# A first stretch unrolled and re-ordered, low weight halves on GpSimd, nine experts' weights prepared beside the first attention groups

## What is computed

```python
x  = L0_attn_x                         # 4 x 1024 x 256, float32: 4096 tokens
xn = layernorm(x)
# attention: 16 heads of 16, causal, q/k/v/o projections with biases
# experts: for each token the 4 best of 16 experts, and 2 shared ones (sw_*: 352 = 2 x 176 columns)
g = einsum('th,ehi->tei', xn, w_gate)  # 16 x 256 x 176
u = einsum('th,ehi->tei', xn, w_up)
y = einsum('tei,eih->th', silu(g) * u * combine, w_down)    # 16 x 176 x 256
y = y + silu(xn @ sw_gate) * (xn @ sw_up) @ sw_down
return x + attention(xn) + y
```

## Time and profile before

| | |
|---|---|
| median of 3 runs | 1188.08 us |
| the profiled execution, its own time | 1197.33 us |
| its span | 1195.7 us |
| PE busy | 1002.8 us (84%) |
| DVE busy | 867.1 us (73%) |
| ACT busy | 654.7 us (55%) |
| POOL busy | 584.0 us (49%) |
| mean granted TensorE clock | 0.934 of full |

### The profile page before, as it was taken

The page is one execution under the profiler, slowest core; times in us unless marked ns, Lnnn a source line. Parts: engine busy times, 40 slices in busy tenths (PEclk is TensorE's granted clock), DMA queues, the critical chain, the costliest instruction groups (busy, mean ns, idle before and its releaser), DMA issues.

```text
span 1195.7 us, 26395 instructions
## 1 busy us (share of the span) xinstructions
PE 1002.8 (84%) x8634; PEld 523.0 (44%) x8634; DVE 867.1 (73%) x1790; ACT 654.7 (55%) x1219; POOL 584.0 (49%) x529
## 2 busy tenths in 40 slices
PE   2877515998989899999998989898989898999875
PEld 1444302444444444554444445444444454444433
DVE  5988687887887767677868776777777766677433
ACT  4777500544545665557666755566666554666431
POOL 6433217777660555346665643565656534544000
PEclk9998755999999999999999999999999998999888
DMA  5998726223242435354544444544444435344602
GB/s 168 286 302 278 233 78 194 62 69 88 68 120 69 97 67 106 52 111 75 107 85 98 87 87 76 91 89 92 78 95 82 99 52 102 58 100 58 136 1 35
DMA packets 99484, 126.41 MB, mean 106 GB/s; under 512 B 24873, under 2 KB 83514, under 8 KB 98834
## 3 DMA queue, kind: packets, MB, share of 16 engines
q0 software_dynamic: 41632, 60.79, 28.4%
q1 hardware_dynamic: 57730, 63.99, 18.0%
HBM read 71.63 MB, written 57.80 MB: 108 GB/s over the span
## 4 chain that ended last, share of the span: by engine, by line
PE 59%; DVE 12%; issue 7%; ACT 2%; SPq 2%; DMA 2%; POOL 0%; ACTq 0%; DVEq 0%
PE gup L1231 12%; PE pvp L1154 12%; PE outs L1258 10%; DVE part L1324 7%; PE smp L1110 6%; PE turn L1243 5%; PE stp L1135 4%; PE outs L1161 4%; PE turn L1201 3%; PE smp L1093 1%; DVE sg L1376 1%; DVE hf L1381 1%; ACT probs L1494 1%; DMA Qs<-nm 1%; DVE probs L1423 1%
## 5 line engine op out<-in xcount | busy, mean ns | idle before, releaser
L1494 ACT ACTIVATE probs<-stp 128x1024 f32<-128x1024 f32 (+1 forms) x320 | 300.1, 938 | 276.6 <-PE stp L1135 267.9
L1324 DVE TENSOR_REDUCE part<-smp 128x2 f32<-128x256 f32 (+2 forms) x372 | 345.8, 950 | 49.5 <-PE smp L1093 30.6
L1231 PE MATMUL gup<-gu_w,XC 128*128 (+1 forms) x1152 | 213.3, 323 | 13.4 <-DVE hf L1381 13.0
L952 POOL DMA_INDIRECT XG<-xrow_d,slots x144 | 147.1, 1022 | 81.6 <-issue 40.2
L959 POOL DMA_INDIRECT out<-Y,slots x72 | 117.2, 1628 | 137.6 <-ACT Y L1527 112.3
L1258 PE MATMUL outs<-dn_w,h 88*128 (+1 forms) x1248 | 183.0, 280 | 0.1
L959 POOL DMA_INDIRECT acc_d<-Y,slots x72 | 115.1, 1599 | 119.5 <-ACT Y L1527 100.9
L1154 PE MATMUL pvp<-probs,Vs 128*32 128x512 f32 (+3 forms) x1536 | 167.8, 509 | 0.8 <-DVE probs L1423 0.7
L941 POOL DMA_INDIRECT slot_d<-entry,slot_i x128 | 129.2, 1009 | 42.5 <-issue 42.5
L1110 PE MATMUL smp<-Ks,Qs 48*128 48x128 f16 (+2 forms) x744 | 112.3, 340 | 38.7 <-DVE part L1324 21.6
L1386 DVE TENSOR_TENSOR h<-turn,h 88x256 f16<-88x256 f32 x208 | 86.6, 417 | 78.3 <-ACT h L1506 77.0
(11 more groups left out here) (174 smaller groups left out, 1138.2 us busy)
## 6 DMA issues: line engine op xcount, KB each, us to landing
rb<-rsum_d SPq DMA_DIRECT2D x60, 128.0 KB
Ks<-k_d SPq DMA_DIRECT2D x96, 64.0 KB
Qs<-q_d SPq DMA_DIRECT2D x96, 64.0 KB
v_d<-V SPq DMA_DIRECT2D x8, 544.0 KB, 5.1
Vs<-v_d SPq DMA_DIRECT2D x16, 272.0 KB, 3.3
acc_d<-YA SPq DMA_DIRECT2D x1, 4224.0 KB
X<-L_attn_x POOLq DMA_DIRECT2D x8, 512.0 KB, 4.8
xrow_d<-XR SPq DMA_DIRECT2D x8, 512.0 KB, 5.0
```

The costliest lines, as they stand in the source:

```text
L952: pool.indirect_dma_start(XG[:, q].rearrange("p a c t -> p (a c t)"), None, s.xrow_d, bass.IndirectOffsetOnAxis(ap=slots[:, r, 0:1], axis= ...
L1231: last = pe.matmul(gup[:, 0:2 * I], columns[:, a, h], weights_of(s.gu_w, e, b, h, slice(0, 2 * I)), start=n == 0, stop=n == 5)
L1324: last = dve.tensor_reduce(part[:, g % 2, k0 // CH, :, j, t], banks[:, :, col:col + w], AX.X, ALU.max)
L1494: act.activation(to, of, ACT.Exp, scale=float(DK) ** -0.5 / QS ** 2).then_inc(exp_done, 1)
```

## The change

- **Order in `prepare`.** All eight chunks are written out; there is no loop. Rows are normalised two chunks ahead and variances taken three ahead: `normalise(c+2)` and `rows_low(c+2)`, and at the end of step `c` `variances(c+3)` on DVE and `root(c+3)` on ACT. Rows 0 and 1 and the variances of 2 stand ahead of the first step. ACT's first work is now the scaling of Wq and Wk; `root(0)` comes behind it.
- **Weights in `prepare`.** Only `s.EARLY` = 7 experts and the 2 shared ones, one expert a step (`c - 1` in step `c`), at the end of ACT's step. The low halves are made by POOL with four instructions in place of DVE's two.
- **The other nine** (`LATER`) are prepared in the third stage, one every five slots, from slot 2 on: SP loads each into the space of `XG` or `YA`, ACT makes the high halves and DVE the low halves. `XG` and `YA`, and the first routed unit on PE, wait for the last of them (`wlo_done`).
- The clearing of `Ks` (one memset of 128x6144 on POOL before) is cut into six of 1024 elements, three in steps 0 and 1 and three in steps 6 and 7.

```diff
@@ prepare, gpsimd @@
+            def weights_low(e, n, k):
+                (gh, gl), (dh, dl) = expert_parts(e)
+                pool.wait_ge(hi_made, 2 * k + 1)
+                pool.tensor_scalar(gu[:, n], gu[:, n], WS, None, ALU.mult).then_inc(scaled, 1)
+                pool.wait_ge(hi_made, 2 * k + 2)
+                pool.tensor_scalar(dn[:, n], dn[:, n], WS, None, ALU.mult).then_inc(scaled, 1)
+                pool.wait_ge(scaled, 2 * k + 1)
+                pool.tensor_tensor(gl, gu[:, n], gh, ALU.subtract).then_inc(lo_made, 1)
+                pool.wait_ge(scaled, 2 * k + 2)
+                pool.tensor_tensor(dl, dn[:, n], dh, ALU.subtract).then_inc(lo_made, 1)
...
-            pool.memset(s.Ks[:, :, :, :], ONES).then_inc(k_ones, 1)
+            def step(c):
+                if c + 4 < NCH:
+                    load_x(c + 4)
+                if c < 2 or c >= NCH - 2:
+                    for b in range(c % 2, NB, 2):
+                        pool.memset(s.Ks[:, b, 0 if c < 2 else 1], ONES).then_inc(k_ones, 1)
+                if c == 0:
+                    for n in range(SH):
+                        weights_low(E + n, n, n)
+                else:
+                    weights_low(c - 1, (c - 1) % 2, c + 1)
+                for e in (range(2) if c == 0 else (c + 1,) if c + 1 < s.EARLY else ()):
+                    pool.wait_ge(lo_made, 2 * (e + 1))
+                    load_expert(e % 2, s.w_gate[e], s.w_up[e], s.w_down[e])
@@ prepare, scalar @@
-            def step(c, p, first, last):
-                product(c, 0)
-                product(c, 1)
-                if more(p, last):
-                    root(c + 1)
-                    rows_high(c + 1, 1 - p)
-                weights_high(c, 0)
-                product(c, 2)
-                product(c, 3)
-                if more(p, last):
-                    columns(c + 1, 1 - p)
+            def step(c):
+                for i in range(4):
+                    product(c, i)
+                if later(c, 2) is not None:
+                    rows_high(c + 2)
                 act.wait_ge(lg_done, c + 1)
...
+                if later(c, 1) is not None:
+                    columns(c + 1)
+                if c == 0:
+                    for n in range(SH):
+                        weights_high(E + n, n, 1)
+                else:
+                    weights_high(c - 1, (c - 1) % 2, (c - 1) // 2 + 2)
+                if later(c, 3) is not None:
+                    root(c + 3)
...
-            root(0)
             act.wait_ge(w_in, 48)
...
             act.activation(w16[:, 2, 0], w32[:, 2], ACT.Copy, scale=WS).then_inc(w_hi, 1)
+            root(0)
+            rows_high(0)
+            columns(0)
+            root(1)
+            rows_high(1)
             act.wait_ge(gt_out, 1)
             act.activation(g16[:, 0], gT32[:, :, :], ACT.Copy, scale=WS).then_inc(w_hi, 1)
+            root(2)
@@ prepare, vector @@
+            def step(c):
+                ahead = later(c, 2) is not None
                 low_half(c, 0)
+                if ahead:
+                    normalise(c + 2)
+                for i in range(1, 4):
+                    low_half(c, i)
+                if ahead:
+                    rows_low(c + 2)
                 values(c, 0)
                 values(c, 1)
+                if later(c, 3) is not None:
+                    variances(c + 3)
@@ attention_and_experts @@
+        WEIGHTS_FROM, WEIGHTS_STEP = 2, 5
+        LATER = E - s.EARLY
+        def weights_at(g, n, half):
+            k = g * SLOTS + n - WEIGHTS_FROM - 2 * half
+            return k // WEIGHTS_STEP if k >= 0 and k % WEIGHTS_STEP == 0 and k // WEIGHTS_STEP < LATER else None
@@ gpsimd, ahead of the first gather @@
+            pool.wait_ge(wlo_done, 2 * LATER)
@@ sync: load_weights(0) ahead of send_max(0), then at the end of a slot @@
+                    e = weights_at(g, n, 0)
+                    if e is not None and e + 1 < LATER:
+                        load_weights(e + 1)
@@ vector, in a slot behind the unit's work (scalar: the same with n, and weights_high) @@
+                    for half in range(2):
+                        if weights_at(g, n - 1, half) is not None:
+                            weights_low(weights_at(g, n - 1, half), half)
```

More of the change, by code:

```diff
@@ L206, in flat, with one, expert_parts, later @@
             return w.rearrange("p c n -> p (c n)")
[L208 to L221, removed]
+        def one(t):
+            return t.rearrange("p o c n -> p (o c) n")
+        def expert_parts(e):
+            e = slice(e, e + 1) if isinstance(e, int) else bass.ds(e, 1)
+            return ([one(s.gu_w[:, e, a]).rearrange("p c (a i) -> p c a i", a=2) for a in range(2)],
+                    [one(s.dn_w[:, e, a]) for a in range(2)])
+        def later(c, ahead):
+            return c + ahead if c + ahead < NCH else None
         @block.sync
@@ L266, in _ @@
-            over_steps(sp, step)
+            for c in range(2):
+                store_rows(c)
+            for c in range(NCH):
+                step(c)
             sp.wait_ge(wo_in, 16 * (4 * HG + 1))
-            sp.wait_ge(xr_st, 16 * NCH)
-            sp.wait_ge(xt_st, 16 * NCH)
+            for p in range(2):
+                sp.wait_ge(xr_st[p], 8 * NCH)
+                sp.wait_ge(xt_st[p], 8 * NCH)
             for i in range(4):
@@ L522, in _, with turn @@
             dve.tensor_scalar(bqk[:, :, :], bqk[:, :, :], QS, None, ALU.mult).then_inc(b_scaled, 1)
+            variances(2)
             dve.wait_ge(v_ones, 1)
-            rows_low(0, 0)
-            for n in range(SH):
-                weights_low(None, n)
-            over_steps(dve, step)
+            for c in range(NCH):
+                step(c)
         @block.tensor
         def _(pe):
-            def turn(c, p):
+            def turn(c):
                 for j in range(TPC):
                     pe.wait_ge(xlo, TPC * c + j + 1)
-                    if j == 0 and not (isinstance(c, int) and c == 0):
+                    if j == 0 and c:
                         pe.wait_ge(xt_done, TPC * c)
@@ L540, in turn, with step @@
                             last = pe.transpose(tp[j // 2][:, j % 2, o:o + P],
-                                                XR[:, p, j, a, h * P:(h + 1) * P], s.ident16[:, :])
+                                                XR[:, c % 2, j, a, h * P:(h + 1) * P], s.ident16[:, :])
                     last.then_inc(turned, 1)
-            def step(c, p, first, last):
-                began = not (isinstance(c, int) and c == 0)
+            def step(c):
+                p = c % 2
                 pe.wait_ge(xt_done, TPC * (c + 1))
@@ L557, in step @@
                     x.then_inc(qk_done, 1)
-                if more(p, last):
-                    turn(c + 1, 1 - p)
-                if began:
+                if later(c, 1) is not None:
+                    turn(c + 1)
+                if c:
                     pe.wait_ge(lg_out, c)
@@ L584, in _ @@
             last.then_inc(gt_done, 1)
-            turn(0, 0)
             pe.wait_ge(w_lo, 4)
-            over_steps(pe, step)
+            for c in range(NCH):
+                step(c)
 def route(nc, s):
@@ L1540, in _ @@
                         second_half(z)
+                    for half in range(2):
+                        if weights_at(g, n, half) is not None:
+                            weights_high(weights_at(g, n, half), half)
 _INS = ["L0_attn_x", "L0_attn_Wq", "L0_attn_bq", "L0_attn_Wk", "L0_attn_bk", "L0_attn_Wv", "L0_attn_bv",
```

210 lines of the change are left out of this document (103 added, 107 removed).

## The result

| | before | after |
|---|---|---|
| median | 1187.76 us (6 runs, 1181.78 to 1190.33) | 1203.76 us (6 runs, 1198.43 to 1209.56) |
| the profiled execution | 1197.33 us | 1202.95 us |
| its span | 1195.7 us | 1201.0 us |

The ratio is 1.0134, 95% interval 1.0104 to 1.0165: the changed kernel is 16 us slower. The forecast was 1189, no change. All ratios in this document are of fast executions; one execution of experiment 3, of 2291 us, is left out of its ratio.

A forecast was written before the change was run, and what follows sets the result against it. DVE was taken to bound the first stage, PE the third with DVE close behind. -6 and +7 gave +1 on the profiled 1197.33 us, in proportion to the median 1189 us, no change; range 1178 to 1200.

The forecast's parts named there:

- -6 for the first stage: First stage: 4.3 us gained in steps 1 to 5, 4.3 in step 6, 0.3 lost in step 7, 2.5 at the start.
- 0.7 on average: Steps 1 to 5: `re_` on DVE waits 0.7 us a step for POOL's arithmetic, upper case 2.
- rival C: First stage: POOL's lock holds `re_` and DVE's subtractions, steps 14.5 to 15 us, nothing gained there; 1195 us, chance 0.12.
- The end stays: End of the first stage: the store of v and the barrier take as long as before.
- Steps 1 to 5: First stage: 13.4 us for each of these steps, 67.0 against 71.3, so 4.3 us gained.
- The root chain: Steps 1 to 5: statistics, then ACT's root, delay the first q/k product; PE waits 1.85 us for a bank.
- Steps 6 and 7: First stage: step 6 takes 11.0 us against 15.3, having neither root nor rows; step 7 PE's 9.0 plus 0.3.
- The start: Start of the first stage: root's end near 16.1 us, first q/k product at 28.1 against 25.58, 2.5 lost.
- The third stage: Nine late experts cost 7 us: 5 on DVE, 1 on ACT, 1 for SP's issues; bounds 1 and 14.
- the first 45 slots take the same time as before: Third stage: a sign that the forecast is wrong; it expected PE idle about 17 us and groups of 65 us.
- 40% of DVE's: Third stage: the share of DVE's added 12.6 us for nine late experts taken as cost, 5 us.
- D: First stage: the root chain doesn't bind, a step is PE's 11.2 to 12 us, 12 to 15 gained; 1182, chance 0.15.

The follow-up runs named there:

- experiment 3: The kernel before, with the nine late experts prepared a second time in the third stage, same values: 1192.24 us, ratio 1.004.
- experiment 1: The changed kernel with the early experts' low halves back on DVE and no arithmetic on POOL: 1177.48 us, ratio to before 0.9916.
- experiment 4: Low halves on DVE as in experiment 1, with ACT's root behind the second q/k product and DVE's normalising behind the second subtraction: 1170.74 us, ratio 0.9863.
- Experiments 5 and 6: Experiment 5 has its own line; 6 is experiment 4 plus four POOL memsets of an unused tile where the changed kernel has its arithmetic: 1188.07 us, ratio 1.0009.
- Experiment 5: The changed kernel, low halves still on POOL, with experiment 4's order of root and normalising: 1197.42 us, ratio 1.0078.

## Why the prediction was wrong, by its own steps

The forecast was -6 for the first stage and +7 for the third. The profiles show +7.9 for the first; the third's share was measured at +5 (1 to 9). Together 13 of the 16 us; the rest is inside the interval of the ratio (12 to 20 us). The two profiled executions alone are 5 us apart: from the first maxima to the end the one before took 998.3 us, the changed one 995.7. Single executions of one kernel differ by some 10 us, so these two don't measure the third stage.

**The step that failed: "since one of 704 elements is nearer to DVE's 0.8 for that shape I take 0.7 on average".** That is the term for POOL's arithmetic, 3.5 us in all, put on one instruction, `re_`. The runs put POOL's arithmetic at 25.2 us (experiment 1 against the changed kernel). Three things in that step were wrong.

- The size. POOL does not take DVE's time for the shape. An expert is 6.6 us on POOL, against 1.4 on DVE. The estimate that I had from the Trainium skill's page GPSIMD Engine Reference, section 3.1, 1.5 us for the subtraction of 704, was right (1.51 measured), and I left it out of the sum. The scaling, which no row priced, took more, 1.97.
- The victims. I looked for one instruction that might meet POOL. POOL's 6.6 us cover nearly half of a step, so something is always hit: the first subtraction, `nw`, `XN`. `re_`, the one that I priced, lost 1.8 us in steps 1 to 5, of 19.0 in all. Even the 0.44 that I took for an undisturbed `re_` was not that: by itself it takes 0.17 (experiment 4). The prediction even quoted the rule for the rest. The Trainium skill's page SBUF — State Buffer, section Who interferes with whom, says that a DVE instruction with two inputs in SBUF contends with a GpSimd instruction that reads SBUF and not with one that only writes it; I gave it to rival C with 0.12. Experiments 5 and 6 agree with it in both halves: 1090 ns beside arithmetic, 683 beside fills.
- The end of the stage. "The end stays" was wrong by 4.9 us: the last expert's 6.1 us on POOL start only when PE is done (140.34), and the barrier waits for them.

**Steps 1 to 5**: forecast 67.0, came 79.2 (39.88 to 119.11). Without POOL's arithmetic they are 61.3 (39.93 to 101.21), where the forecast without its 3.5 would be 63.5. The root chain is real but smaller: PE waits 1.01 us for the third product, not 1.85 (experiment 1). So of the 12.2 us that were missing, POOL's arithmetic is 14.4 (17.9 instead of 3.5), and an overpriced rest gave 2.2 back, unplanned.

**Steps 6 and 7**: forecast 11.0 and 9.3, came 11.4 and 9.0. Right.

**The start**: forecast 28.1 for the first product, table load of 1.28 near 15 and root's end at 16.1; came 27.59, 14.29 and 15.79. Right. What I missed is step 0, which had been 15.3 us (25.58 to 40.91) and became 12.3, since its rows are ready too: 3.0 gained that I had not counted, so that step 1 starts 1 us earlier than before and not 2.5 later.

These add up: 12.2 on steps 1 to 5, 0.4 and -0.3 on steps 6 and 7, 4.9 at the end, -3.5 on start and step 0, together 13.7, the distance from -5.8 to +7.9.

**The third stage**: 7 was taken, 5 measured, within the bounds of 1 and 14, but with an interval of 1 to 9 that doesn't part the two. PE's idle time in the 140 us rose from 9.8 to 12.9 us, not to 17, and groups did not become 65 us long. One sign that the prediction set itself, that the first 45 slots take the same time as before, did come: in the profiled executions they do. Over groups 0 and 1 only 0.5 us of idle time was added, 2.1 in experiment 3. This points to a sizing by "40% of DVE's" that was too high; where the rest of the 5 us lies isn't shown.

**The rivals**: C was the right one in its mechanism (the lock, DVE's subtractions included, steps of 14.5 to 15: they are 14.7 from the third on) and in sign. It lacked the shared experts in step 1 and the end of the stage; step 1 is 4.4 us longer than the later ones and the end 4.9, and with both its 1195 would have been about 1204. That this is the measured median is in part luck: C also lacked the 3.5 us gained at the start and in step 0. D was wrong for this kernel, whose steps are 14.7. Without POOL's arithmetic its 11.2 to 12 us a step did come (11.9), but not its reason, since PE still waited 1 us for the root chain.

## What to carry to other kernels

An instruction moved from VectorE to GpSimd has two prices: its own time there (here 6.6 us for what took 1.4), and the time in which it holds VectorE's instructions of the kinds that were held here (`tensor_scalar`, and `tensor_tensor` with both operands in SBUF; the statistics were not). VectorE was busy for most of the stage, and the second price came to 2.1 to 2.8 us for each later step with 6.6 us of arithmetic in it, more where two experts stood together, and 4.9 at the end. So it does not help to look for the one small instruction that may be hit. A place for GpSimd's work where VectorE has gaps was not tried. Of this change, what paid was the deeper lead of the rows and the experts moved to the third stage (0.9916), and then the root and the normalising out of the way of the products that wait for them (0.9863).

## What the runs showed of the hardware that was not expected

- On GpSimd the scaling by a constant, with one input, was slower than the subtraction with two: 1.97 us against 1.51 for 128x704 float32 input, 1.54 against 1.45 for 88x512 on average. The scaling writes float32 and the subtraction float16; whether that is why isn't shown.
- When GpSimd's instructions follow each other without a gap, VectorE can be held over more than one of them. Experiment 5, VectorE first, then GpSimd:

```profile
76.77 2.48 DVE L450 TENSOR_SCALAR re_<-mv 128x4 f32<-128x4 f32 x1
```

```profile
76.27 1.48 POOL L279 TENSOR_SCALAR dn_stage<-dn_stage 88x512 f32<-88x512 f32 x1
77.72 1.51 POOL L281 TENSOR_TENSOR gu_w<-gu_stage,gu_w 128x704 f16<-128x704 f32 x1
```

  `re_` starts at 76.77, GpSimd's first ends at 77.75, and yet `re_` ends at 79.25, with GpSimd's second (79.23). So one instruction can cost more than the longest instruction beside it, which I had taken for the upper bound.
- GpSimd's issuing of a DMA can hold a small VectorE instruction as well. Before the change, `re_` took 0.42 to 0.44 us in four of steps 1 to 5 and 0.17 in the other. In the four it ended together with the issue beside it, as in the earlier trace rows, where it ran from 87.60 to 88.04:

```profile
87.34 0.70 POOL L282 DMA_DIRECT2D gu_stage<-L_ffn_w_up  x1
```

- Of the changed kernel, the two executions at a granted clock of 0.932 took 1208 and 1210 us, those at 0.938 and 0.939 took 1204 and 1198: a difference in clock of 0.7% goes with up to 1% of the time, as much as many changes are worth. The clock isn't all of it, since those at 0.933 and 0.936 took 1203 and 1204 as well. Times of single executions are to be read with their clock.
